# Sixty kept edge groups in place of sixty-six in the four-head graph attention sums

## The chip, the cores and the metric

The kernel runs on one core of a Trainium2 chip. The core has a matrix engine (PE, with its weight loads as PEld), a vector engine (DVE), a scalar engine (ACT), a general engine (POOL) and a queue engine (SP). SP, ACT and POOL can issue transfers, and all transfers share 16 DMA engines. The metric is the device time of one execution in microseconds, as the median of several runs. Lower is better.

## The reference

Two graph layers run over 3125 nodes and 50000 edges, sorted by destination. Each has an attention over edges, a linear attention over all nodes and a mixture of experts. The change touches the first attention pass of the second layer, which has four heads of 128 columns:

```python
h = (x @ W).reshape(N, heads, out_c)
a_src = jnp.einsum('nhc,hc->nh', h, att_src)
a_dst = jnp.einsum('nhc,hc->nh', h, att_dst)
e = jax.nn.leaky_relu(a_src[src] + a_dst[dst], NEG_SLOPE)
...
msg = h[src] * alpha[:, :, None]
out = jax.ops.segment_sum(msg, dst, num_segments=N)
```

For every edge a row of `h` is fetched by the edge's source, scaled by the edge's weight for each head, and added into the row of the edge's destination. Four heads of 128 columns and one more column each make a row of 516 floats, 2064 bytes.

## The kernel before

The edges stand in 196 blocks of 256. A block can span several tiles of 128 destination nodes, so the work is cut into `W` = 220 edge groups (block and tile; called w in the code), and each has two halves of 128 edges (`SUB` = 2). The sum of one group is a matrix product: a one-hot matrix of destinations (128 edges by 128 nodes) times the 128 scaled rows, done for two halves and two banks of 261 columns, and added to the tile's accumulator in SBUF.

The rows of a group come into SBUF by one of two ways.

- **Direct rows.** POOL issues two indirect gathers (L1616, one for each half of 128 rows) from `table1` in DRAM within the sums themselves.
- **Kept rows.** For the groups in the list `STAGED`, POOL issues the same two gathers earlier, in other stages (L1173), and a queue writes the rows as one dense block of 516 KB to `kept1` in DRAM (L1183). In the sums SP reads that block back with one plain transfer (L1604).

`STAGED` holds the groups with w % 10 in (2, 5, 8), 66 of 220. The first `FIRST` = 16 of them are gathered and stored in the linear attention of this layer, those up to `EARLY` = 56 (40 groups) in the score stage, and the remaining 10 in the softmax stage. In each of these stages five buffers (`KQ`) turn over: POOL's gather of group n waits until the store of group n - 5 has landed.

The stages run one after another with a barrier between them. Those that matter here, in order:

1. The score stage, `edge_scores_l1`. For 110 pairs of edge groups SP loads a block of one-hot matrices (`hots`, 128 KB, ten buffers), PE multiplies, DVE masks (L1315) and reduces (L1321). Beside it POOL gathers kept groups and ACT's queue stores them.
2. The softmax stage, `segment_softmax`, with 10 more kept groups.
3. The sums, `aggregate`. POOL issues the direct gathers in group order into `QD` = 7 slots; a slot is free once PE has summed the group that held it. SP loads kept blocks into `QS` = 3 slots. ACT writes five more columns into each group's rows (L1640) and scales the second half by the edge weights (L1644). DVE writes the one-hot matrices (L1668, `QH` = 5 buffers), scales the first half (L1673) and adds PE's result to the accumulator (L1682). PE multiplies (L1659).

In the sums POOL, SP, ACT and PE have straight code for 220 groups. DVE runs a loop (L1692) with `J1` = 20 groups in its body, since the tile of a group is only known at run time. The order of DVE's work is written out: one-hot and message of group w + 2, then the addition of group w. `J1` has to be a multiple of the period of `STAGED`, and the counts per turn of the body of both slot rings have to come out whole; that is where the constants 2 * 16 in `landed` come from.

Of the kernel before, what the change touches and what calls it, by code (L numbers as in the profile page):

```python
# [36 lines left out]
W = NB + NT - 1  # L37
SUB = EB // P
# [11 lines left out]
H1, DH1 = 4, 128  # L50
# [4 lines left out]
WSP = 448  # L55
C0, C1, C2 = 16, 32, 112
ROW0 = H0 * (DH0 + 1)
J1 = 20
STAGED = [w for w in range(W) if w % 10 in (2, 5, 8)]
FIRST = {H1: 16, 1: 0}  # L60
EARLY = {H1: 56, 1: 58}
KQ = 5
STAGED_B = [b for b in range(NB) if b % 3 == 1]
RING = 37
# [1091 lines left out]
def staged(H):  # L1156
    return STAGED if H == H1 else STAGED_B

# [5 lines left out]
def gather_rows(pool, K, table, rows, windows, s_free, sources=None):  # L1164

    Q = rows.shape[1]
    sources = K.src_col if sources is None else sources
    for n, w in enumerate(windows):
        q = n % Q
        if n >= Q:  # L1170
            pool.wait_ge(s_free[q], 16 * (n // Q))
        for s in range(SUB):
            pool.indirect_dma_start(rows[:, q, s, :], None, table,  # L1173
                                    bass.IndirectOffsetOnAxis(ap=sources[:, w * SUB + s:w * SUB + s + 1], axis=0)).then_inc(K.gath[q], 16)
# [19 lines left out]
def edge_scores_l1(prog, K, name, H, C, RW, table, kept, A):  # L1194
# [4 lines left out]
    with Stage(prog, name) as st:  # L1199
# [30 lines left out]
        turns = W // (G * QL)  # L1230
        first, early = FIRST[H], EARLY[H]
        L = WSP // C * P
# [147 lines left out]
def segment_softmax(prog, K, name, H, C, keep_max=None, RW=0, table=None, kept=None, A=None):  # L1380
# [8 lines left out]
    with Stage(prog, name) as st:  # L1389
# [18 lines left out]
        s_free = [st.sem(f"free{q}") for q in range(KQ)]  # L1408
        early, late = (EARLY[H], len(staged(H)) - EARLY[H]) if table is not None else (0, 0)
        if late:  # L1410
# [147 lines left out]
def aggregate(prog, K, name, H, RW, table, kept, acc, extra):  # L1558
# [4 lines left out]
    B = 1 if RW <= 512 else 2  # L1563
    part = -(-(RW + X) // B)
    with Stage(prog, name) as st:
        U2, QH, J = 4, 5, J1
        QS, QD = 3, 7
        size = SUB * B * part
        HALF = 1 if B > 1 else SUB
        al = K.al[:, 0:WS * H].rearrange("p (s h) -> p s h", h=H)  # L1570
# [7 lines left out]
        s_gath, gathered = K.gath, list(K.gathered)  # L1578
        s_rows = [st.sem(f"rows{q}") for q in range(QS)]
# [5 lines left out]
        if by_act:  # L1585
            away = st.sbuf("away", [P, 2, SUB, P])
            one = st.sbuf("one", [P, 1])
        direct = [w for w in range(W) if w not in STAGED]
        rows, landed = {}, {}
        for n, w in enumerate(direct):  # L1590
            rows[w] = slots[n % QD]
            landed[w] = (s_gath[n % QD], gathered[n % QD] + 16 * SUB * (n // QD + 1), 2 * 16 * SUB)
        for n, w in enumerate(STAGED):
            rows[w] = slots[QD + n % QS]
            landed[w] = (s_rows[n % QS], 16 * (n // QS + 1), 2 * 16)
        per_ready = 1 if by_act else 2
        block = st.block()

        @block.sync
        def _(sp):  # L1600
            for n, w in enumerate(STAGED):
                if n >= QS:
                    sp.wait_ge(s_sum, STAGED[n - QS] + 1)
                sp.dma_start(rows[w][:, :, 0:RW], kept[n * EB:(n + 1) * EB, :].rearrange("(s p) r -> p s r", p=P)).then_inc(s_rows[n % QS], 16)  # L1604
# [775 lines left out]
def linear_attention_l1(prog, K, A):  # L2380

    KD = LH * LD
    with Stage(prog, "mix1") as st:
# [33 lines left out]
        def _(pool):  # L2417
            st.clear_stale(pool)
            gather_rows(pool, K, K.table1, held, STAGED[0:FIRST[H1]], s_free)

# [581 lines left out]
def stages(prog, K, A, out):  # L3002

    order_edges(prog, K, A)
    items_project_l0(prog, K, A)
    linear_attention_l0(prog, K, A)
    edge_scores_l0(prog, K, A)
    segment_softmax(prog, K, "soft0", H0, C0, A=A)
    aggregate_l0(prog, K)
    finish_route_l0(prog, K, A)  # L3010
    experts_l0(prog, K, A)
    join_project_l1(prog, K, A)
    linear_attention_l1(prog, K, A)
    for H, C, RW, table, kept, acc in ((H1, C1, H1 * (DH1 + 1), K.table1, K.kept1, K.acc1),
                                       (1, C2, D + 1, K.table2, K.kept2, K.acc2)):
        keep = K.al[:, WSP * H:WSP * (2 * H + 1)].rearrange("p (s h) -> p s h", h=H + 1)
        edge_scores_l1(prog, K, f"score_h{H}", H, C, RW, table, kept, A)
        segment_softmax(prog, K, f"soft_h{H}", H, C, keep, RW, table, kept)
        if H == H1:
            aggregate(prog, K, f"sum_h{H}", H, RW, table, kept, acc, keep)  # L3020
            middle_l1(prog, K, A)
        else:
            aggregate_one(prog, K, table, kept, acc, keep)
    finish_route_l1(prog, K, A)
    experts_l1(prog, K, A)
    combine_l1(prog, K, out)
# [126 lines left out]
```

## Time and profile before

| What | Value |
| --- | --- |
| Median of three runs | 3053.57 us (3051.1 to 3061.77) |
| The profiled execution | 3050.74 us, its span 3049.0 us |
| PE, share of the span busy | 2105.7 us, 69% |
| DVE | 2085.5 us, 68% |
| POOL | 1440.7 us, 47% |
| ACT | 827.2 us, 27% |
| Score stage, up to its last store | about 1493 to 1640 us from the span's start |
| Softmax stage | about 1665 to 1711 us |
| The sums | about 1711 to 2143 us |

Busy shares of the whole span mix stages with different limits, so the table is only a map. The page's chain of work that ended last covers only the final 44 us of the span and says nothing of these stages. What a change here is worth has to be read from the views of each stage: busy times in a stretch, who waited for whom in it, and the instructions in order of time.

### The profile page before, as it was taken

How to read it: one execution, taken by the hardware profiler on the slowest of the kernel's cores; microseconds unless marked ns; L12 is line 12 of the kernel's file. 1: busy time of each engine (PE TensorE's matmuls, PEld its weight loads, DVE VectorE, ACT ScalarE, POOL GpSimd, SP SyncE). 2: the span in 40 equal slices, each digit the busy share in tenths (PEclk: the TensorE clock that was granted, in tenths of full speed). 3: DMA queues.
4: the chain of work that ended last, by engine and by line, in shares of the span. 5: the costliest groups of instructions: out<-in, count | busy, mean ns of one | idle time of the engine just before them, and what ended most of it. 6: DMA issues, size and time to landing. Idle time of an engine off the chain costs nothing. (4 is left out here: it accounts for less than half of the span.)

```text
span 3049.0 us, 51563 instructions
## 1 busy us (share of the span) xinstructions
PE 2105.7 (69%) x11892; PEld 1580.5 (52%) x11893; DVE 2085.5 (68%) x4524; ACT 827.2 (27%) x2459; POOL 1440.7 (47%) x1486
## 2 busy tenths in 40 slices
PE   2634878757887389948665499999756188887372
PEld 2322434445665355624565377787645177776252
DVE  7496888888888343353478688888677277778442
ACT  2314444431001212124200467676500000001110
POOL 2477777700000310130553777777357677771234
PEclk9866998979998599979777699999856599998586
DMA  4777999935775278843997788898589645550085
GB/s 151 208 205 218 269 269 270 271 139 172 229 232 149 98 256 271 271 125 118 340 393 263 238 278 281 277 287 275 137 285 269 190 130 158 159 148 20 35 257 175
DMA packets 447837, 649.13 MB, mean 213 GB/s; under 512 B 67552, under 2 KB 328286, under 8 KB 447123
## 3 DMA queue, kind: packets, MB, share of 16 engines
q1 hardware_dynamic: 329747, 351.62, 37.0%
q0 software_dynamic: 82640, 248.85, 27.6%
q10 hardware_dynamic: 35296, 46.90, 4.5%
q8 instruction: 61, 1.00, 0.1%
q14 instruction: 93, 0.76, 0.1%
HBM read 478.83 MB, written 169.68 MB: 213 GB/s over the span
## 5 line engine op out<-in xcount | busy, mean ns | idle before, releaser
L1616 POOL DMA_INDIRECT wide<-table,src_col x264 | 277.9, 1053 | 80.7 <-issue 73.3
L1777 PE MATMUL sum_h_ps<-wide,sum_h_hot 128*128 x880 | 254.1, 412 | 75.4 <-DVE wide L1802 45.6
L1037 POOL DMA_INDIRECT arena_b<-table,al x272 | 258.1, 949 | 89.2 <-issue 85.2
L1753 POOL DMA_INDIRECT wide<-table,al x262 | 257.9, 984 | 85.8 <-issue 58.8
L1659 PE MATMUL sum_h_ps<-wide,sum_h_hot 128*128 128x261 f32 x1056 | 253.4, 389 | 37.2 <-ACT wide L1644 21.2
L1885 PE MATMUL sum_ps<-wide,sum_hot 128*128 128x264 f32 x880 | 211.9, 394 | 52.4 <-DVE sum_hot L1895 27.5
L1659 PEld LDWEIGHTS sum_h_ps<-wide,sum_h_hot 128*128 128x128 f32 x1056 | 197.3, 191 | 85.2 <-issue 29.7
L1173 POOL DMA_INDIRECT wide<-table,src_col x132 | 138.6, 1050 | 198.1 <-issue 134.1
L1885 PEld LDWEIGHTS sum_ps<-wide,sum_hot 128*128 128x128 f32 x880 | 163.8, 191 | 100.4 <-issue 74.9
L1058 PE MATMUL score_ps_hd<-wide,score_hot 128*128 x1320 | 209.5, 301 | 0.0
L1777 PEld LDWEIGHTS sum_h_ps<-wide,sum_h_hot 128*128 128x128 f32 x880 | 155.2, 197 | 92.8 <-issue 79.7
L1114 DVE TENSOR_TENSOR wide<-wide,score_ps_hd 128x528 f32<-128x528 f32 x220 | 153.3, 697 | 37.8 <-PE score_ps_hd L1058 32.9
L1899 DVE TENSOR_TENSOR wide<-wide,al 128x528 f32<-128x528 f32 x220 | 154.4, 702 | 32.8 <-DMA wide<-edge_h 32.2
L1068 ACT ACTIVATE wide<-score_ps_en 128x512 f32<-128x512 f32 x220 | 130.5, 594 | 147.6 <-PE score_ps_en L1054 147.1
L1644 ACT ACTIVATE wide<-wide,al 128x129 f32<-128x129 f32 x528 | 167.3, 388 | 0.0
L797 POOL DMA_INDIRECT wide<-table,al x120 | 124.1, 1034 | 91.0 <-issue 90.7
L1659 PE MATMUL sum_h_ps<-arena_b,sum_h_hot 128*128 128x261 f32 x704 | 166.2, 383 | 0.1
L1682 DVE TENSOR_TENSOR wide<-wide,sum_h_ps 128x522 f32 x220 | 152.3, 692 | 19.5 <-issue 13.6
L1054 PE MATMUL score_ps_en<-enc_rows,score_attr 30*128 30x256 bf16 x440 | 91.5, 290 | 104.2 <-DVE score_hot L1107 35.8
L1173 POOL DMA_INDIRECT wide<-table,al x130 | 125.2, 963 | 73.4 <-issue 53.2
L1058 PEld LDWEIGHTS score_ps_hd<-wide,score_hot 128*128 128x128 bf16 x1320 | 118.9, 104 | 72.9 <-issue 52.5
L1973 POOL MEMSET route_ones<- 128x128 f32 x1 | 0.4, 400 | 325.7 <-POOLq L127 325.7
(537 smaller groups left out, 4991.9 us busy)
## 6 DMA issues: line engine op xcount, KB each, us to landing
wide<-edge_h SPq DMA_DIRECT2D x220, 264.0 KB, 3.0
edge_h<-arena_b SPq DMA_DIRECT2D x68, 528.0 KB
arena_b<-kept SPq DMA_DIRECT2D x66, 516.0 KB, 5.2
wide<-edge_rows SPq DMA_DIRECT2D x110, 256.0 KB, 4.7
score_h_hot<-hots SPq DMA_DIRECT2D x220, 128.0 KB
kept<-wide ACTq DMA_DIRECT2D x40, 516.0 KB, 8.5
wide<-kept SPq DMA_DIRECT2D x65, 257.0 KB
wide<-in_f_w SPq DMA_DIRECT2D x16, 1024.0 KB, 10.0
```

What stands on the lines that cost most here:

```text
L1037: pool.indirect_dma_start(rows[:, q, k, :], None, K.table0[:, :], bass.IndirectOffsetOnAxis(ap=K.src_blk[:, g * GS + k:g * GS + k + 1], ax ...
L1058: ins = pe.matmul(ps_hd[:, m, s, 0:D + H], lhsT=hot[:, q, edges[s]], rhs=near[:, window, c, :], start=(c == 0), stop=(c == 2))
L1114: dve.tensor_tensor(prod[:, w % U3, :].rearrange("p (s d) -> p s d", s=SUB), enc[:, m, :].rearrange("p (s d) -> p s d", s=SUB), ps_hd[:, m ...
L1173: pool.indirect_dma_start(rows[:, q, s, :], None, table, bass.IndirectOffsetOnAxis(ap=sources[:, w * SUB + s:w * SUB + s + 1], axis=0)).th ...
L1616: pool.indirect_dma_start(rows[w][:, s, 0:RW], None, table, bass.IndirectOffsetOnAxis(ap=K.src_col[:, w * SUB + s:w * SUB + s + 1], axis=0 ...
L1644: ins = act.activation(cols, cols, ACT.Copy, scale=al[:, w * SUB + 1, h:h + 1])
L1659: ins = pe.matmul(ps[:, u, b, 0:part], lhsT=hot[:, w % QH, s, :], rhs=rows[w][:, s, b * part:(b + 1) * part], start=(s == 0), stop=(s == S ...
L1682: dve.tensor_tensor(out, out, ps[:, j % U2, :, 0:part], ALU.add).then_inc(s_acc, 1)
L1753: pool.indirect_dma_start(ring[:, b % RING, s, :], None, table, bass.IndirectOffsetOnAxis(ap=K.src_blk[:, b * SUB + s:b * SUB + s + 1], ax ...
L1777: pe.matmul(ps[:, u, 0:RW], lhsT=hot[:, q, s, :], rhs=ring[:, bass.ds(places[j % 4], 1), s, :].rearrange("p a r -> p (a r)"), start=(s == ...
L1885: ins = pe.matmul(ps[:, bass.ds(banks[j % 4], 1), 0:ROW0].rearrange("p a c -> p (a c)"), lhsT=hot[:, q, s, :], rhs=rows[:, q, s, :], start ...
L1899: dve.tensor_tensor(view, view, al[:, bass.ds(w * SUB, SUB), :].unsqueeze(3).broadcast_to([P, SUB, H, R]), ALU.mult).then_inc(s_msg, 1)
```

## The change

The list of kept groups becomes w % 11 in (2, 6, 9), 60 groups. `FIRST` stays 16, `EARLY` becomes 50, so that the score stage keeps 34 groups in place of 40 and the softmax stage still 10. The sums have 160 direct groups in place of 154, eight direct slots in place of seven, and four one-hot buffers in place of five. The loop body of DVE covers 44 groups in place of 20.

```diff
-J1 = 20
-STAGED = [w for w in range(W) if w % 10 in (2, 5, 8)]
+J1 = 44
+STAGED = [w for w in range(W) if w % 11 in (2, 6, 9)]
 FIRST = {H1: 16, 1: 0}
-EARLY = {H1: 56, 1: 58}
+EARLY = {H1: 50, 1: 58}
...
-        U2, QH, J = 4, 5, J1
-        QS, QD = 3, 7
+        U2, QH, J = 4, 4, J1
+        QS, QD = 3, 8
...
-            landed[w] = (s_gath[n % QD], gathered[n % QD] + 16 * SUB * (n // QD + 1), 2 * 16 * SUB)
+            landed[w] = (s_gath[n % QD], gathered[n % QD] + 16 * SUB * (n // QD + 1), 4 * 16 * SUB)
...
-            landed[w] = (s_rows[n % QS], 16 * (n // QS + 1), 2 * 16)
+            landed[w] = (s_rows[n % QS], 16 * (n // QS + 1), 4 * 16)
```

POOL's row of instructions at the score stage, as a piece of the difference (x80 means eighty in a row, two for each group):

```order
 L1261 UNCONDITIONAL_BRANCH
 L120 ISA
-L1173 DMA wide<-table,src_col 128x516 x80
+L1173 DMA wide<-table,src_col 128x516 x68
 L127 UNCONDITIONAL_BRANCH
 L1433 UNCONDITIONAL_BRANCH
```

Twelve gathers have left the score stage; ACT's queue has 34 stores there in place of 40 (L1183).

POOL's row at the start of the sums, before the change (`wide` holds six of the direct slots, `arena_b` the rest):

```order
L120 ISA
L1611 MEMSET wide 128x2 x6
L1611 MEMSET arena_b 128x2 x4
L1616 DMA wide<-table,src_col 128x516 x12
L1616 DMA arena_b<-table,src_col 128x516 x2
```

And after it:

```order
L120 ISA
L1611 MEMSET wide 128x2 x6
L1611 MEMSET arena_b 128x2 x5
L1616 DMA wide<-table,src_col 128x516 x12
L1616 DMA arena_b<-table,src_col 128x516 x4
```

A turn of the slots is now 16 gathers for eight groups in place of 14 for seven; the pattern goes on to 320 gathers in place of 308. SP's row at the same stage has 60 loads of kept blocks (L1604) in place of 66. The work of DVE, ACT and PE for a group is the same and in the same order; the loop of DVE, from its first instruction to its branch back, is 472 instructions long in place of 220.

## Rows read from the trace of the kernel before

**Rows 1.** Busy us of the engines (and counts) in stretches: scores, their end, softmax, sums
```profile
core 0: us, PE busy (x) PEld busy (x) DVE busy (x) ACT busy (x) POOL busy (x), PEclk, DMA share, GB/s
...
1493.00:1640.00 147.00, 94.73 (x1479) 85.14 (x1478) 114.94 (x193) 0.00 (x0) 76.77 (x80) 0.73 1.04 385
1640.00:1665.00 25.00, 14.06 (x298) 13.16 (x296) 24.26 (x57) 0.00 (x0) 0.00 (x0) 0.84 0.31 98
1665.00:1712.00 47.00, 13.13 (x48) 6.59 (x46) 25.97 (x21) 11.47 (x24) 31.99 (x30) 0.50 0.71 225
1712.00:2143.00 431.00, 401.07 (x1760) 330.38 (x1760) 362.26 (x661) 297.40 (x1101) 328.65 (x308) 0.98 0.86 271
```

**Rows 2.** Groups of POOL in the sums: busy us, mean ns, idle before, releasers
```profile
L1616 POOL DMA_INDIRECT wide<-table,src_col x264 | 277.9, 1053 | 80.7 <-issue 73.3 <-PE sum_h_ps L1659 7.3
L1616 POOL DMA_INDIRECT arena_b<-table,src_col x44 | 50.7, 1153 | 13.4 <-issue 11.6 <-PE sum_h_ps L1659 1.8
```

**Rows 3.** The line of the direct gathers: ns min/median/max, first and last start
```profile
L1616 POOL DMA_INDIRECT wide<-table,src_col x264: 942/948/6483, 1712.3 to 2130.4; - x132
L1616 POOL DMA_INDIRECT arena_b<-table,src_col x44: 942/1241/1450, 1733.5 to 2133.6; - x44
```

**Rows 4.** Waits of POOL in the sums: total us, times, longest us
```profile
POOL wide L1616 <- issue: 73.3, 240, 0.5
...
POOL wide L1616 <- PE sum_h_ps L1659: 7.3, 24, 0.3
```

**Rows 5.** Waits of DVE in the sums
```profile
DVE wide L1673 <- DMA wide<-table,src_col: 44.1, 52, 4.3
...
DVE sum_h_hot L1668 <- issue: 3.4, 1, 3.4
```

**Rows 6.** Sums in order of time, five instructions: start us, us, engine, operation
```profile
1711.30 6.68 DVE L1687 TENSOR_TENSOR wide<-eps 128x6264 f32<-128x6264 f32 x1 [16.69 <-DMA wide<-edge_h]
...
1712.33 6.48 POOL L1616 DMA_INDIRECT wide<-table,src_col  x1 [0.53 <-issue]
...
1915.15 0.94 POOL L1616 DMA_INDIRECT wide<-table,src_col  x1 [0.30 <-issue]
...
1924.03 0.69 DVE L1673 TENSOR_TENSOR arena_b<-arena_b,al 128x516 f32<-128x516 f32 x1
...
1924.29 1.24 POOL L1616 DMA_INDIRECT arena_b<-table,src_col  x1 [0.30 <-issue]
```

**Rows 7.** The end of the sums in order of time: last gather, last addition
```profile
2133.57 0.95 POOL L1616 DMA_INDIRECT arena_b<-table,src_col  x1 [0.30 <-issue]
...
2141.45 0.70 DVE L1682 TENSOR_TENSOR wide<-wide,sum_h_ps 128x522 f32 x1 [0.91 <-PE sum_h_ps L1659]
```

**Rows 8.** The group of POOL's gathers in the score stage, as in Rows 2
```profile
L1173 POOL DMA_INDIRECT wide<-table,src_col x80 | 76.8, 960 | 72.3 <-DMA kept<-wide 47.1 <-issue 14.3 <-POOLq L127 10.9
```

**Rows 9.** POOL in the score stage in order of time: first and last gather
```profile
1493.44 0.94 POOL L1173 DMA_INDIRECT wide<-table,src_col  x1 [10.86 <-POOLq L127]
...
1630.74 0.95 POOL L1173 DMA_INDIRECT wide<-table,src_col  x1 [0.30 <-issue]
```

**Rows 10.** The longest wait of PE in the score stage, from 1493 to 1640 us
```profile
PE score_h_ps L1293 <- DMA score_h_hot<-hots: 38.2, 54, 1.5
```

**Rows 11.** DVE's masks in order of time: 1, 91, 92 and 110 of 110
```profile
1511.90 0.62 DVE L1315 TENSOR_TENSOR wide<-score_h_ps,arena_b 128x448 f32<-128x448 f32 x1 [1.59 <-PE score_h_ps L1295]
...
1639.42 0.62 DVE L1315 TENSOR_TENSOR wide<-score_h_ps,arena_b 128x448 f32<-128x448 f32 x1
...
1640.57 0.62 DVE L1315 TENSOR_TENSOR wide<-score_h_ps,arena_b 128x448 f32<-128x448 f32 x1
...
1659.60 0.62 DVE L1315 TENSOR_TENSOR wide<-score_h_ps,arena_b 128x448 f32<-128x448 f32 x1
```

**Rows 12.** Transfers from 1493 to 1640 us: all; stores: count, KB, us to landing
```profile
DMA packets 31543, 56.56 MB, mean 385 GB/s; under 512 B 3504, under 2 KB 16244, under 8 KB 31401
...
kept<-wide ACTq DMA_DIRECT2D x40, 516.0 KB, 8.5
```

## The prediction, made before the run

> **What bounds the kernel now.** The page's chain of waits ends in the last 44 us, so I read the two stages that the change touches one by one: busy times in stretches [rows 1], then who waited in each, then single instructions. The reader should look for the engine that never rests.
>
> In the sums that is POOL. Its gathers run from 1712.33 to 2133.57 + 0.95 = 2134.52 us [rows 6, 7], 422.2 us for 308. Their busy time is 277.9 + 50.7 = 328.6 us, and the idle time ahead of them 80.7 + 13.4 = 94.1 us [rows 2]; together 422.7, the whole stretch. The idle time is no wait: it is 0.305 us ahead of every gather, and where PE's freeing of a slot is named as releaser it is never over 0.3 us either [rows 4]. So POOL issues without a pause, and slots never hold it up. The others wait for it: DVE 44.1 us for rows that have not landed [rows 5]. PE is busy 401 of 431 us [rows 1], but busy PE is pipelined and modelled, and DVE's and PE's last work ends 7.6 us behind POOL's last gather (2141.45 + 0.70 against 2134.52 [rows 7]), as a short pipeline behind its source would. The sums last as long as their gathers.
>
> A gather takes 0.948 us in the median [rows 3], with the gap 1.253. The mean is longer: 328.6 - 308 x 0.948 = 36.6 us are on top. How shows in the order of time [rows 6]: the first gather starts while DVE clears the accumulator (L1687, until 1717.98) and takes 6.48 us, ending after it; the one at 1924.29 starts 0.26 us into a message multiply (L1673) and takes 1.24; the one at 1915.15 has none beside it and takes 0.94. So gathers that start inside certain DVE operations are held: 5.5 us in the first, 31 us spread over the other 307, or 0.10 each.
>
> In the score stage the transfers are full: share 1.04, 385 GB/s, until 1640 us, then 0.31 [rows 1]. PE waits 38.2 us for the blocks of one-hot matrices [rows 10], and DVE, which ends the stage, waits for PE. When stores and gathers are over, DVE runs without a pause: 18 masks from 1640.57 to 1659.60, 1.057 us each; before that 90 masks took 1511.90 to 1639.42, 1.417 us each [rows 11].
>
> **The change part by part.**
>
> *Twelve gathers more in the sums.* 160 direct groups in place of 154, two gathers each: 12 x 1.253 = 15.0 us on the path that sets the stage's end. Nothing hides them, for POOL has no pause. The holds I leave at their 36.6 us in all: they come from 220 message multiplies, whose number stays, and as groups come more slowly a gather is less likely to start inside one. If the holds went by gathers, the mean of the 307, (422.2 - 6.8) / 307 = 1.353, would hold: 16.2 us. Downwards, fewer holds could take back at most those 31 us (a rival below). I take +15.0, with 12 to 17 as its near bounds.
>
> The Trainium skill ("SBUF — State Buffer", section "Who interferes with whom") says that a DVE instruction with two SBUF inputs contends with a GpSimd instruction that reads SBUF, and adds, as inferred, that tensor_tensor was not seen to stall transfers issued by GpSimd. The held gathers here agree with the first and speak against the second. By the first the holds belong to DVE's work and the term is 15.0; by the second they would be the gathers' own and it would be 16.2.
>
> *Six kept groups less in the score stage.* 80 gathers become 68, 40 stores 34. POOL waits there for stores (47.1 us [rows 8]), and 40 groups take 1493.44 to 1631.69, 3.46 us each [rows 9]; six less end 20.7 us earlier. In these 20.7 us DVE goes at 1.057 instead of 1.417 us a pair: the gain is 20.7 x (1 - 1.057 / 1.417) = 5.3 us. It cannot be less than nothing, since only work leaves. As upper bound, the bytes: six groups read and stored are 6 x 2 x 516 KB = 6.3 MB, at 385 GB/s [rows 12] 16.5 us, if all of that became the stage's. I take -5.3, since the last 19 us of the stage are already at DVE's own pace and cannot shrink.
>
> *Six loads less on SP, the same bytes in all.* A load of a kept group is replaced by gathers of the same rows; SP waits for slots only. Nothing is queued behind it. 0.
>
> *Ten late groups in the softmax stage* (1665 to 1712 us [rows 1]) and 16 early ones stay in number. 0.
>
> *Eight direct slots, four one-hot buffers.* POOL was never held by seven slots, so an eighth gives nothing. DVE writes the one-hot of group w + 2 after the addition of w - 1, when PE is through with w - 1 and all before; the fourth buffer back held w - 2. No wait is added. 0; the one memset more costs less than a gather's gap.
>
> *The loop body of 472 instructions in place of 220.* The trace shows one stall of DVE's instruction supply, 3.4 us at the entry of the loop, and none at its branches back [rows 5]. A body of the new length isn't in the trace, so each of the three branches back (four turns in the loop) costs between 0 and 3.4 us of DVE, 10.2 in all. DVE isn't the bound, though. What a late DVE delays is a slot's release. Eight slots turn over in 16 x 1.353 = 21.6 us; a slot is needed from its first gather to its group's addition, about 1.25 + (2141.45 - 2133.57) = 9.1 us by the last group [rows 7]. Some 12 us of cover hide 3.4. 0; if the cover is gone, 10.2.
>
> **The sum.** 15.0 - 5.3 = +9.7 us. On the profiled execution (3050.74 us; span 3049.0) this gives 3060.4; that execution lies 2.8 below the median of the runs (3053.57), from which it gives 3063.3. I put the median at 3062.
>
> A difference of about 0.3%, 9.2 us, is what a measurement of this kernel can tell from no change. The forecast, slower, stands right on that line.
>
> **The rivals.**
>
> *The score stage gives back all its bytes (not slower).* Place: PE's wait for one-hot blocks. With the transfers full until 1640, 6.3 MB less might bring the whole stage forward 16.5 us: 15.0 - 16.5 = -1.5, on the scale of the 3062 above 3051. It decides when the stores end later than DVE's last wait, so that DVE's free stretch stays 19 us long. For it: the share of 1.04. Against: DVE has to do its 110 pairs at 1.057 or more whatever the transfers do, and blocks gain only as much as DVE loses now.
>
> *DVE's loop stalls at each turn and the cover does not hold (slower).* 3 x 3.4 = 10.2 us on top: 3072. Part of it may come another way: a DVE that catches up has its multiplies closer together and holds more gathers. For it: the stall at entry. Against: the cover above. The Trainium skill ("Runtime: NRT & Kernel Launch", section "Instruction fetch mechanics") says that an engine keeps two pages of 256 instructions, fetched in sequence, and that a taken branch out of them waits for a fetch. The old body fits in one page, the new one takes both; no trace so far shows which way this falls.
>
> *The holds go away (faster).* The starts of gathers fall differently against the multiplies; if all 31 us vanished, 15.0 - 31 - 5.3 = -21.3, 3031; half of them, 3046. For it: 0.94 is the time of a gather that is left alone. Against: nothing in the change takes multiplies away or shifts them.
>
> *The sums do not follow the gathers.* If PE sets the pace, twelve more gathers fill pauses, and only the score stage counts: 3062 - 15.0 = 3047. Against: POOL has no pauses.
>
> **How the numbers follow.** The sum as worked out: 66%, with some 4 us either way, so it falls about evenly on the two sides of the line: 36% slower by over 0.3%, 30% within. Score stage gives back all: 12%, within. Loop stalls: 13%, slower. Holds go away: 5%, faster. Sums not bound by gathers: 4%, within. Faster 5%, within 46%, slower 49%. The range of 3053 to 3070 leaves out the holds, most of the score stage's full return, half of the loop's stalls, some 2 in 10.
>
> **What would show it.** In the profile after: 320 gathers in the sums with idle gaps of 0.3 us and no long wait for PE, from first to last some 437 us; a median of 0.95 us; DVE still waiting for landed rows. The score stage's last gather some 20 us nearer its first, and DVE's free stretch at 1.06 us some 35 masks long in place of 19. DVE idle for instructions once, or four times, at the loop. The prediction is wrong if gathers wait for slots, if the score stage shortens by far more than 5 us, or if the mean gather is no longer about 1.06 us.

## The result: slower by 0.6%, and what the profile after shows

| | kernel before | changed kernel |
|---|---|---|
| median of 11 runs of each, us | 3046.17 (3033.96 to 3061.77) | 3065.7 (3056.51 to 3072.87) |
| ratio, 95% interval | | 1.0059 (1.0039 to 1.0078) |
| profiled execution, its span, us | 3050.74, 3049.0 | 3062.84, 3061.1 |
| score stage, us | 172.1 | 165.6 |
| softmax stage, us | 46.6 | 46.7 |
| sums, us | 432.0 | 462.0 |

A stage is counted from its own start to the start of the next (POOL's first instruction in each, L120). By the ratio the change costs 0.0059 x 3046 = 18 us, where 9.7 were forecast. In the two profiled executions the score stage gives back 6.5 us and the sums cost 30. The stages that the change doesn't touch are 11.5 us shorter together (30.0 - 6.5 + 0.1 - 12.1) in this one execution of the changed kernel; over the 14 profiles of this study the time ahead of the score stage runs from 1488.2 to 1496.0 us and that behind the sums from 898.6 to 907.1, and this execution lies at the low end of both. So sizes in whole are taken from the medians and places from the profiles.

The changed kernel by stretches, as in [rows 1]: scores while POOL gathers, the rest of the scores, softmax, sums.

```profile
core 0: us, PE busy (x) PEld busy (x) DVE busy (x) ACT busy (x) POOL busy (x), PEclk, DMA share, GB/s
1488.00:1617.00 129.00, 87.95 (x1327) 80.95 (x1328) 101.98 (x170) 0.00 (x0) 68.17 (x68) 0.68 1.03 382
1617.00:1654.00 37.00, 22.19 (x451) 19.93 (x448) 36.26 (x80) 0.00 (x0) 0.00 (x0) 0.91 0.31 91
1654.00:1700.00 46.00, 13.25 (x48) 6.69 (x47) 25.39 (x20) 10.74 (x23) 31.63 (x20) 0.50 0.71 230
1700.00:2162.00 462.00, 411.10 (x1760) 336.23 (x1760) 367.04 (x661) 300.43 (x1101) 355.05 (x331) 0.96 0.82 253
```

The score stage did what the forecast said. Its first and last gather, and three of VectorE's masks (the first, the 77th and the 110th), in order of time:

```profile
1489.07 0.94 POOL L1173 DMA_INDIRECT wide<-table,src_col  x1 [10.29 <-POOLq L127]
...
1506.67 0.62 DVE L1315 TENSOR_TENSOR wide<-score_h_ps,arena_b 128x448 f32<-128x448 f32 x1 [1.59 <-PE score_h_ps L1295]
...
1603.51 0.94 POOL L1173 DMA_INDIRECT wide<-table,src_col  x1 [0.30 <-issue]
...
1613.82 0.61 DVE L1315 TENSOR_TENSOR wide<-score_h_ps,arena_b 128x448 f32<-128x448 f32 x1
...
1648.70 0.62 DVE L1315 TENSOR_TENSOR wide<-score_h_ps,arena_b 128x448 f32<-128x448 f32 x1
```

From first to last gather 114.4 us against 137.3 before [rows 9]. The last 34 masks run without a pause, (1648.70 - 1613.82) / 33 = 1.057 us apart, the same pace as the last 19 before [rows 11].

The sums did not. The two groups of POOL's gathers, as in [rows 2]:

```profile
L1616 POOL DMA_INDIRECT wide<-table,src_col x240 | 269.5, 1123 | 73.3 <-issue 65.7 <-PE sum_h_ps L1659 7.6
L1616 POOL DMA_INDIRECT arena_b<-table,src_col x80 | 85.1, 1064 | 24.4 <-issue 23.2 <-PE sum_h_ps L1659 1.2
```

The idle time is 73.3 + 24.4 = 97.7 us for 320 gathers, still 0.305 each: POOL issues without a pause as before, and no wait for a slot appears. But a gather takes 354.6 / 320 = 1.108 us in the mean where it took 1.067. I call *held time* what the gathers after the first take beyond 0.945 us each (the first starts in VectorE's clearing of the accumulator and is 5.2 to 5.5 us over in each kernel): 354.6 - 302.4 - 5.2 = 47.0 us, where rows 2 give 32.0 in the same way. So the 30 us are 12 x 1.25 = 15 for the gathers, and 15 for holds that were forecast to stay.

VectorE's waits in the sums, as in [rows 5], name the second thing that is new:

```profile
DVE wide L1673 <- DMA wide<-table,src_col: 43.6, 43, 4.4
...
DVE sum_h_hot L1668 <- issue: 16.2, 4, 4.8
```

It now stalls for instructions four times, 16.2 us, where it stalled once for 3.4: at the entry and at each of three branches back. In order of time, around the first branch back (L1673 is the message multiply, L1668 the one-hot):

```profile
1802.39 0.69 DVE L1673 TENSOR_TENSOR wide<-wide,al 128x516 f32<-128x516 f32 x1
...
1807.34 0.95 POOL L1616 DMA_INDIRECT wide<-table,src_col  x1 [0.30 <-issue]
1808.29 0.42 DVE L1668 TENSOR_TENSOR sum_h_hot<-iota_row,rel_col 128x256 f32<-128x256 f32 x1 [4.31 <-issue]
...
1820.47 0.69 DVE L1673 TENSOR_TENSOR arena_b<-arena_b,al 128x516 f32<-128x516 f32 x1
1820.51 1.46 POOL L1616 DMA_INDIRECT wide<-table,src_col  x1 [0.30 <-issue]
...
1822.24 0.69 DVE L1673 TENSOR_TENSOR arena_b<-arena_b,al 128x516 f32<-128x516 f32 x1
1822.28 1.46 POOL L1616 DMA_INDIRECT wide<-table,src_col  x1 [0.30 <-issue]
```

During the stall the gathers run free and POOL loses nothing. It loses later: multiplies follow each other every 1.77 us, one gather starts 0.04 us into each of them and takes 1.46 us in place of 0.945. Eleven such steps stand in a row from 1816.9 us on. There are four rows of steps of 1.74 to 1.80 us in the trace, at 1816.9, 1905.2, 1997.5 and 2104.3 us, of 11, 10, 11 and 5 steps; the first three each begin 12 to 15 us after the start of the multiply step that the stall lengthened. The four hold gathers for 18.5 us of the 47.0. The trace of before has no row of three or more.

### The profile page after: what moved, and what is told of

Its sections match the earlier page's. It is cut to its first block and busy times, and to the rows that moved or that the text cites. A ratio compares the mean times of both kernels' runs of the same rounds, so it can differ in the third digit from the quotient of the medians.

```text
span 3061.1 us, 51420 instructions
## 1 busy us (share of the span) xinstructions
PE 2108.4 (69%) x11892; PEld 1586.4 (52%) x11893; DVE 2091.6 (68%) x4524; ACT 828.7 (27%) x2459; POOL 1456.1 (48%) x1487
## 5 line engine op out<-in xcount | busy, mean ns | idle before, releaser
L1616 POOL DMA_INDIRECT wide<-table,src_col x240 | 269.5, 1123 | 73.3 <-issue 65.7
L1659 PE MATMUL sum_h_ps<-wide,sum_h_hot 128*128 128x261 f32 x960 | 233.8, 394 | 44.2 <-ACT wide L1644 21.0
L1659 PEld LDWEIGHTS sum_h_ps<-wide,sum_h_hot 128*128 128x128 f32 x960 | 183.2, 194 | 89.0 <-DVE wide L1673 34.1
L1173 POOL DMA_INDIRECT wide<-table,src_col x120 | 130.0, 1084 | 199.0 <-issue 148.4
L1777 PEld LDWEIGHTS sum_h_ps<-wide,sum_h_hot 128*128 128x128 f32 x880 | 155.4, 197 | 91.6 <-issue 78.7
L1659 PE MATMUL sum_h_ps<-arena_b,sum_h_hot 128*128 128x261 f32 x800 | 192.2, 390 | 13.8 <-DVE arena_b L1673 11.7
L1058 PE MATMUL score_ps_hd<-wide,score_hot 128*128 x1320 | 201.5, 293 | 0.0
L1659 PEld LDWEIGHTS sum_h_ps<-arena_b,sum_h_hot 128*128 128x128 f32 x800 | 153.0, 193 | 43.8 <-DVE arena_b L1673 17.5
L1119 DVE TENSOR_REDUCE al<-wide 128x16 f32<-128x528 f32 x220 | 153.0, 696 | 0.0
## 6 DMA issues: line engine op xcount, KB each, us to landing
score_h_hot<-hots SPq DMA_DIRECT2D x220, 128.0 KB, 12.3
```

Source lines behind the costliest of these rows:

```text
L1058: ins = pe.matmul(ps_hd[:, m, s, 0:D + H], lhsT=hot[:, q, edges[s]], rhs=near[:, window, c, :], start=(c == 0), stop=(c == 2))
L1119: dve.tensor_reduce(al[:, w * SUB:(w + 1) * SUB, :], prod[:, w % U3, :].rearrange("p (s h r) -> p s h r", s=SUB, h=H), AX, ALU.add).then_i ...
L1173: pool.indirect_dma_start(rows[:, q, s, :], None, table, bass.IndirectOffsetOnAxis(ap=sources[:, w * SUB + s:w * SUB + s + 1], axis=0)).th ...
L1616: pool.indirect_dma_start(rows[w][:, s, 0:RW], None, table, bass.IndirectOffsetOnAxis(ap=K.src_col[:, w * SUB + s:w * SUB + s + 1], axis=0 ...
L1659: ins = pe.matmul(ps[:, u, b, 0:part], lhsT=hot[:, w % QH, s, :], rhs=rows[w][:, s, b * part:(b + 1) * part], start=(s == 0), stop=(s == S ...
L1777: pe.matmul(ps[:, u, 0:RW], lhsT=hot[:, q, s, :], rhs=ring[:, bass.ds(places[j % 4], 1), s, :].rearrange("p a r -> p (a r)"), start=(s == ...
```

## The experiments

Each kernel was run beside the kernel before; a ratio is against that. For the sums, the length of the stage and the held time in one profiled execution are given.

| kernel | groups kept, form of VectorE's loop | sums, us | held, us | ratio, 95% interval |
|---|---|---|---|---|
| before | 66, turns of 20 | 432.0 | 32.0 | 1 |
| after | 60, turns of 44 | 462.0 | 47.0 | 1.0059 (1.0039 to 1.0078) |
| before_body40 | 66, turns of 40 | 444.3 | 44.3 | 1.0025 (1.0010 to 1.0040) |
| before_straight | 66, no loop | 451.8 | 51.7 | 1.0050 (1.0032 to 1.0068) |
| list_straight | 60, no loop, 7 slots, 5 one-hots | 458.2 | 41.2 | 1.0066 (1.0048 to 1.0084) |
| after_straight | 60, no loop | 463.7 | 49.1 | 1.0070 (1.0042 to 1.0097) |
| after_gaps | 60, no loop, 3 pauses put in | 463.7 | 49.6 | 1.0070 (1.0049 to 1.0092) |
| after_short | 60, turns of 44, multiply cut | 425.1 | 4.1 | one execution, 3036.6 us |
| before_psum | 66, no loop, weights in PSUM | 407.7 | 5.0 | 0.9905 (0.9886 to 0.9924) |
| after_psum | 60, no loop, weights in PSUM | 422.2 | 5.6 | 0.9922 (0.9906 to 0.9938) |
| after_pad256 | 60, no loop, 0.34 us more work a group | 437.7 | 20.4 | 0.9988 (0.9976 to 1.0000) |
| after_pad128 | 60, no loop, 0.20 us more work a group | 470.9 | 56.8 | 1.0097 (1.0073 to 1.0121) |
| before_loads | 66, no loop, register loads added | 495.6 | 30.7 | 1.0197 (1.0178 to 1.0215) |
| after_loads | 60, no loop, register loads added | 496.4 | 29.7 | 1.0181 (1.0162 to 1.0200) |

The score stage takes 161.7 to 167.7 us in the kernels with 60 groups kept and 170.6 to 172.5 in those with 66.

### Is it the loop? Straight code, pauses, and a long body on the old list

after_straight takes the loop out of VectorE's part of the sums:

```diff
-            turns = W // J
-            with aligned(dve, 0, turns - 1) as i:
-                for j in range(J):
-                    message(i + (j + 2) // J, (j + 2) % J)
-                    add(i, j)
...
+            for w in range(W):
+                if w + 2 < W:
+                    message(0, w + 2)
+                add(0, w)
```

> The changed kernel with DVE's 220 groups in the sums written out as straight code, so that no branch back is left. Loop theory: the 472-instruction body stalls DVE 4.3 to 5.0 us at each of its three branches back; DVE then runs without a pause at PE's pace, and POOL's gathers start inside its message multiplies one after the other. Without the branches the sums fall from 462 us to 445 to 455, holds from 47 us (without the first gather) to 32 to 38, and the whole stands at +0.1 to +0.4% of before. Rival, the pattern: the holds come with 3 of 11 and 320 gathers whatever the loop does; the sums stay at 458 to 462 us and the whole at +0.6%.

Sums 463.7 us, held 49.1, ratio 1.0070: no stall is left, and nothing is won. As far as this run went, the loop was cleared.

after_gaps is after_straight with a reduction into a tile that nobody reads (4.8 us) behind groups 43, 87 and 131, so that VectorE pauses where the loop would branch.

```diff
...
+                if w in (43, 87, 131):
+                    dve.tensor_reduce(idle[:, :], K.al[:, 0:1480].unsqueeze(1).broadcast_to([P, 3, 1480]), AX, ALU.max)
...
```

> As the changed kernel with straight code, but with three reductions of about 4.6 us on DVE (one input, result unused) after groups 43, 87 and 131, where the loop branched back. If lateness of DVE is what costs, by its catching up, the sums are as long as with the loop, 455 to 462 us, though no instruction is fetched anew. If the fetch itself costs (its transfers, or the branch), the sums are as with straight code alone, 445 to 455 us.

463.7 us and 49.6 held, longer than either view had expected: three pauses add nothing to straight code, which already had as many holds. But the pauses do make rows. Behind the first one (L1674 is the multiply here):

```profile
1808.93 4.78 DVE L1697 TENSOR_REDUCE sum_h_idle<-al 128x3 f32<-128x4440 f32 x1
...
1824.82 0.69 DVE L1674 TENSOR_TENSOR arena_b<-arena_b,al 128x516 f32<-128x516 f32 x1
1824.86 1.47 POOL L1617 DMA_INDIRECT wide<-table,src_col  x1 [0.30 <-issue]
```

Rows of 9, 10 and 11 steps begin at 1821.3, 1909.1 and 2009.1 us, at groups 50, 93 and 142, where the changed kernel's begin at groups 50, 93 and 138; after_straight has no row near them. VectorE takes no branch here, so being late is enough to start a row. The total stays because other holds go: gathers in steps of 1.5 to 1.6 us hold 8.0 us in place of 14.3.

before_body40 puts the long body on the old list: 66 groups kept, seven slots, five one-hot buffers, turns of 40 groups in place of 20.

```diff
-J1 = 20
+J1 = 40
...
-            with aligned(dve, 0, turns - 1) as i:
+            with aligned(dve, 0, 4) as i:
...
+            for w in range(4 * J, W):
+                if w + 2 < W:
+                    message(0, w + 2)
+                add(0, w)
...
```

> The kernel before (66 kept groups, 308 gathers) with DVE's loop body of 40 groups in place of 20, four turns, the last 60 groups as straight code. Loop theory: three branches back stall 4 to 5 us each, the gathers after each are held, and the sums grow from 432 us by 7 to 15. Rival, the pattern: no stall that matters, sums 430 to 434 us, whole within 0.1% of before.

It stalls at its branches back like the changed kernel and is slower by 0.25%, 7.6 us; sums +12.3 us, held time 44.3, also +12.3. So one part of the change, alone, brings four fifths of the 15 us of new holds. One thing goes with the long body: the last 60 groups are straight code, where before has 20 and the changed kernel 44. Of the 12.3 us, 8.5 fall in the first 160 groups and 3.7 in those 60. Its waits and its order of time:

```profile
DVE sum_h_hot L1668 <- issue: 14.9, 4, 4.1
```

```profile
1885.32 0.43 DVE L1668 TENSOR_TENSOR sum_h_hot<-iota_row,rel_col 128x256 f32<-128x256 f32 x1 [4.09 <-issue]
...
1890.59 0.69 DVE L1673 TENSOR_TENSOR arena_b<-arena_b,al 128x516 f32<-128x516 f32 x1
1890.86 1.25 POOL L1616 DMA_INDIRECT wide<-table,src_col  x1 [0.30 <-issue]
...
1892.14 0.70 DVE L1673 TENSOR_TENSOR wide<-wide,al 128x516 f32<-128x516 f32 x1
1892.41 1.24 POOL L1616 DMA_INDIRECT wide<-table,src_col  x1 [0.30 <-PE sum_h_ps L1659]
...
1898.45 0.69 DVE L1673 TENSOR_TENSOR wide<-wide,al 128x516 f32<-128x516 f32 x1
1898.61 1.35 POOL L1616 DMA_INDIRECT wide<-table,src_col  x1 [0.30 <-issue]
...
1901.98 0.69 DVE L1673 TENSOR_TENSOR arena_b<-arena_b,al 128x516 f32<-128x516 f32 x1
1902.03 1.47 POOL L1616 DMA_INDIRECT wide<-table,src_col  x1 [0.30 <-issue]
```

Here the holds can be read as a rule. A gather that starts 0.27 us into a multiply takes 1.25 us (0.30 held), at 0.16 us it takes 1.35 (0.40), at 0.05 us 1.47 (0.52). Start and hold add up to 0.57 us each time: **the gather goes on when 0.57 of the multiply's 0.69 us have passed**. Over all 172 gathers of after_straight that start in a multiply the means agree: 0.49 held for starts at 0.05 to 0.10 us, 0.30 at 0.20 to 0.30, 0.01 from 0.50 on. (Of the starts in the first 0.03 us none is held, from 0.04 us on all of them are: the gather that comes first is let through.)

From this follows when the next gather starts, wherever in the multiply the held one began: 0.57 + 0.945 + 0.305 = 1.82 us after the multiply's start (median in the trace of after 1.813, over the 128 gathers held by more than 0.05 us). If the next multiply starts sooner than that, the gather falls into it, and it is held too unless it comes in the first 0.03 us. That puts the boundary near 1.82 - 0.03 = 1.79 us, and the eleven traces with the whole multiply and both inputs in SBUF bear it out: behind a held gather the next one is held in all 541 steps of 1.5 to 1.78 us, in 44 of 51 from 1.78 to 1.79, and in 1 of 26 from 1.79 to 1.82. **Multiplies in step at under 1.79 us keep the gathers in step with them: one gather for each, at the multiplies' pace, in place of one each 1.25 us.** The hold is then what the step has over 1.25 us: VectorE catching up has steps of 1.55 us (0.30 held), VectorE waiting for TensorE steps of 1.77 us (0.51 held; in the rows TensorE ends a group every 1.766 us, and each addition starts 0.16 us behind it). The chain ends when the landed rows are used up and a multiply has to wait. A stall of 4 us is what starts a long one: three or four gathers land unhindered meanwhile, VectorE then has rows in store, and goes without landing waits for 14 to 18 groups.

Neither view of the loop had it whole: it does cost, in long turns; straight code, which has no stalls, gets as many holds from somewhere else.

### Do the multiplies hold the gathers?

after_short is the changed kernel with the multiply cut to the first column of each head; the other columns of that half stay unweighted.

```diff
-                view = rows[j][:, 0:HALF, 0:RW].rearrange("p s (h r) -> p (s h) r", h=H)
+                view = rows[j][:, 0:HALF, 0:RW].rearrange("p s (h r) -> p (s h) r", h=H)[:, :, 0:1]
...
```

> The changed kernel with its loop, the message multiply of DVE cut to the first column of each head (128 x 4 in place of 128 x 516), so that 128 of 129 columns of each group's first half stay unscaled. If gathers are held by this multiply, its holds shrink with its length (0.69 us to about 0.1): mean gather 0.95 to 1.0 us, 320 x 1.26 = 403 us from first to last, sums 415 to 430 us. If they are held by anything else (ring space, full transfers), the mean stays at 1.07 to 1.1 us and the sums at 445 us or more.

Held time 4.1 us with 320 gathers, sums 425.1 us: the multiply it is. But it takes work away too, so the next pair doesn't. before_psum and after_psum copy the head weights once into two spare PSUM banks (three PSUM pairs for the sums in place of four); the multiply is as long as before and has one input in SBUF, not two. Both are in straight code.

```diff
-        U2, QH, J = 4, 5, J1
+        U2, QH, J = 3, 5, J1
...
+        hw = st.psum("hw", [P, 1024])
...
-                dve.tensor_tensor(view, view, al[:, bass.ds(w * SUB, HALF), :].rearrange("p s h -> p (s h)").unsqueeze(2).broadcast_to([P, HALF * H, RW // H]),
+                dve.tensor_tensor(view, view, weights(w, 1).unsqueeze(2).broadcast_to([P, HALF * H, RW // H]),
...
+            for k in range(4):
+                dve.tensor_copy(weights(60 * k, min(60, W - 60 * k)).rearrange("p (s h) -> p s h", h=H), al[:, 120 * k:min(120 * k + 120, WS):2, :]).then_inc(s_one, 1)
```

> The kernel before in straight code, with the head weights that the message multiply reads copied once into two spare PSUM banks (three PSUM pairs for the sums in place of four), so that the multiply has one SBUF input and one from PSUM; nothing else is changed and nothing is left out. If the holds come from the multiply's two inputs in SBUF, gathers lose nearly all of their 32 us, and the sums end about 20 us earlier, near 410 to 415 us, where TensorE (220 groups of 1.758 us) takes over as the bound. If the holds come from the write of the rows, or from any VectorE work, they stay and the sums stay at 430 us or more.

> The same on the changed kernel (60 kept groups, eight slots, four one-hot buffers). If the holds are gone in both, the difference of the sums to before_psum is the bare price of twelve more gathers: 12 x 1.25 = 15 us where the gathers are the bound, 0 to 5 us where TensorE is. The changed kernel would be at 0 to +9 us against before_psum in whole, since its scores end 6.5 us earlier. If the holds stay, sums 455 us or more.

Both came out as expected, and better. POOL's groups in the sums of before_psum, the sums as one stretch, and a gather that starts 0.17 us into a multiply (L1677 there):

```profile
L1617 POOL DMA_INDIRECT wide<-table,src_col x264 | 259.3, 982 | 80.6 <-issue 71.8 <-PE sum_h_ps L1660 8.8
...
L1617 POOL DMA_INDIRECT arena_b<-table,src_col x44 | 42.3, 962 | 13.4 <-issue 10.4 <-PE sum_h_ps L1660 3.0
```

```profile
1709.00:2117.00 408.00, 391.49 (x1760) 333.78 (x1760) 367.41 (x665) 295.87 (x1101) 301.96 (x318) 0.98 0.88 286
```

```profile
1854.72 0.69 DVE L1677 TENSOR_TENSOR wide<-wide,sum_h_hw 128x516 f32<-128x516 f32 x1
1854.89 0.95 POOL L1617 DMA_INDIRECT arena_b<-table,src_col  x1 [0.30 <-issue]
```

The same start cost 0.40 us in before_body40 and costs nothing here. So it is the second SBUF input of this multiply, not the write and not VectorE being busy. Two SBUF inputs alone don't say how long a hold is: the one-hot has two as well, and 48 gathers that started in it here were held by 0.09 us in the mean. Against its own control, before_straight, the sums fall by 44.1 us; the kernel is 0.95% faster than the kernel before, 27.2 us by medians (3022.83 against 3049.98), and the fastest of this study. With the holds gone the two lists show the bare price: sums 14.5 us longer with twelve more gathers, scores 8.6 shorter, 4.5 us in whole by the medians (3027.34 - 3022.83), though the two intervals overlap.

### What the list costs in straight code

before_straight is the kernel before without the loop, list_straight that with the list of 60 alone.

```diff
-STAGED = [w for w in range(W) if w % 10 in (2, 5, 8)]
+STAGED = [w for w in range(W) if w % 11 in (2, 6, 9)]
...
-EARLY = {H1: 56, 1: 58}
+EARLY = {H1: 50, 1: 58}
...
```

> The kernel before (list, seven slots, five one-hot buffers kept), with VectorE's loop in the sums of the four-head pass written out in full, as in after_straight. It is the control for that run. Theory A, the list itself brings the holds (the message multiplies of eight direct groups in eleven fall behind TensorE's pace, then gathers and multiplies run in step): here the old list is in straight code, so the sums stay at 432 us (+-4), held time of the gathers after the first near 32 us, the time within 0.2% of before. Theory B, what counts is the form of the loop (twenty groups with cheap branches back keep the multiplies out of step, every other form does not): sums near 444 to 450 us, held time 44 us or more, the time 10 to 16 us above before, and of the 18 us of the change only the bare gathers, 5 to 15 us, belong to the list.

> The kernel before with the new list alone (60 kept groups, the scores' count of early groups with it), in straight code; seven slots for direct rows and five one-hot buffers as before. Theory A (list): as after_straight, sums 460 to 466 us, held time 47 to 50 us; slots and one-hot buffers have no part in it. Rival (the four one-hot buffers bring VectorE back into step with TensorE): sums 445 to 450 us, held time 35 to 40 us.

The control fell to theory B: the old list in straight code has 51.7 us of held time, more than the changed kernel, and is 0.5% slower than its own loop of twenty. list_straight met neither of its expectations, with 458.2 us and 41.2 held. Between these two the list costs 3.1 us (3068.6 - 3065.52), less than the intervals can tell from nothing. Slots and one-hot buffers (after_straight against list_straight) can't be told from nothing either.

Where straight code differs from the loop can be read behind a multiply that waited for its rows. In before_straight:

```profile
1861.92 0.70 DVE L1673 TENSOR_TENSOR wide<-wide,al 128x516 f32<-128x516 f32 x1 [0.27 <-DMA wide<-table,src_col]
1862.09 1.34 POOL L1616 DMA_INDIRECT wide<-table,src_col  x1 [0.30 <-issue]
...
1863.70 0.69 DVE L1673 TENSOR_TENSOR arena_b<-arena_b,al 128x516 f32<-128x516 f32 x1
1863.74 1.47 POOL L1616 DMA_INDIRECT wide<-table,src_col  x1 [0.30 <-issue]
```

The step is 1.78 us, under the boundary: one hold leads to the next. In the kernel before the same step is 1.89 us (median of 46), since its addition starts 0.24 us behind such a multiply and not 0.14: the next gather starts in time, ahead of the next multiply. Of these steps 3 of 46 are under 1.79 us in before, 39 of 43 in before_straight.

### Is there such a boundary? More work, less time

If chains need steps under 1.8 us, VectorE must get *slower* to free the gathers. after_pad256 is after_straight with the group's one-hot made a second time into a buffer that nobody reads; after_pad128 makes half of it.

```diff
...
+                if w >= 2:
+                    dve.wait_ge(s_spare, w - 1)
+                dve.tensor_tensor(spare[:, w % 2, 0:2, :], K.iota_row[:, :].unsqueeze(1).broadcast_to([P, 2, P]),
+                                  K.rel_col[:, bass.ds(w * SUB, 2)].unsqueeze(2).broadcast_to([P, 2, P]), ALU.is_equal).then_inc(s_spare, 1)
...
```

> after_straight with work added: ahead of every message multiply VectorE makes the group's one-hot a second time into a scratch buffer that nobody reads (128x256, 0.42 us, of which 0.08 overlaps: 0.34 us more per group, 75 us more VectorE work in all). Theory (step): in all traces a gather that starts s us into a multiply ends s-independently, held until 0.57 us of the multiply have passed (hold = 0.57 - s), so the next gather starts 1.82 us after that multiply's start; it falls into the next multiply, and is held again, only when multiplies follow each other in less than 1.82 us. Catch-up steps of 1.55 and 1.77 us do; with the added work the shortest step is 1.55 + 0.34 = 1.89 us, so chains of held gathers can't form: held time falls from 49 us to 15 or less, and the sums get shorter in spite of the added work, 463.7 -> 435 to 448 us (VectorE 220 x 1.89 = 416 plus 20 to 30 at the ends and waits). Rival (a gather is held the more, the more VectorE works): held time 50 us or more, sums 470 us or more.

> The same with half of the added work: only the first 128 columns of the one-hot are made twice (about 0.28 us, 0.20 us more per group, 44 us more in all). By the step theory the shortest step of the multiplies is then about 1.75 us, still under 1.82: gathers stay in step, each held 1.82 - 1.75 + ... = about 0.5 us, so held time stays at 45 us or more and the sums at 460 us or more: worse than with twice the added work. Rival (added work only loosens VectorE and gathers in proportion): between after_straight and after_pad256.

Gathers (min/median/max ns, by the line of POOL) and the sums as one stretch, after_pad256:

```profile
L1618 POOL DMA_INDIRECT wide<-table,src_col x240: 945/967/6147, 1705.5 to 2125.3; - x120
L1618 POOL DMA_INDIRECT arena_b<-table,src_col x80: 945/967/1585, 1726.5 to 2130.4; - x80
```

```profile
1704.00:2142.00 438.00, 417.76 (x1760) 318.40 (x1760) 425.99 (x881) 297.64 (x1101) 328.45 (x331) 0.98 0.85 267
```

after_pad128, and one step of a chain in it:

```profile
L1618 POOL DMA_INDIRECT arena_b<-table,src_col x80: 942/1370/1465, 1728.9 to 2168.4; - x80
```

```profile
1707.00:2177.00 470.00, 411.46 (x1760) 332.74 (x1760) 405.15 (x881) 300.09 (x1101) 364.65 (x330) 0.97 0.81 248
```

```profile
1841.03 0.69 DVE L1679 TENSOR_TENSOR wide<-wide,al 128x516 f32<-128x516 f32 x1
1841.09 1.44 POOL L1618 DMA_INDIRECT wide<-table,src_col  x1 [0.30 <-PE sum_h_ps L1661]
```

The step theory stands on both sides. With 0.20 us more a group, 102 of 219 steps are under 1.79 us, all but the first of them at 1.75 or more, where a hold is 0.5 us, and the sums lengthen to 470.9; with 0.34 us more, one is, VectorE is busy 426 of 438 us, and the sums are 26 us *shorter* than without any padding. The two runs put the boundary between 1.75 and 1.89 us; the traces above put it at 1.79. Held time of after_pad256 is 20.4 us where 15 or less was expected. 13.4 us of it is one chain of 21 gathers from 2057.45 us on, with steps of 1.885 us and 0.64 us held: its gathers start 0.07 to 0.08 us *ahead* of the multiply, inside the useless one-hot. So a gather can also be caught just before the multiply starts, and a chain run at longer steps. The start alone doesn't decide that: 89 other gathers of this run start equally far ahead at the same steps and take 0.97 to 0.99 us. What sets the 21 apart stays open.

### A test that missed its aim

before_loads and after_loads were to lengthen only the step behind a landing, by reading the register of the addition three times.

```diff
...
-                window = dve.value_load(K.window[0:1, bass.ds(w, 1)], min_val=0, max_val=NT - 1)
+                for again in range(3):
+                    window = dve.value_load(K.window[0:1, bass.ds(w, 1)], min_val=0, max_val=NT - 1)
...
```

> before_straight with the window's register load written three times ahead of each add (two of them useless). In the traces the step from a multiply that waited for its rows to the next one is 1.89 us in the kernel before's loop of twenty groups and 1.78 us in straight code, since the add behind it starts 0.24 us after the multiply in the loop and 0.14 us in straight code; the boundary at which a held gather meets the next multiply is 1.82 us. Step theory: the added loads lengthen that one step past 1.82 us and are hidden elsewhere, so the straight code behaves as the loop did: held time 51.7 -> 28 to 38 us, sums 451.8 -> 428 to 438 us, the time within 0.3% of before. Rival (the step after a landing doesn't matter; straight code is worse for another reason): held time 45 us or more, sums 448 us or more.

> The same on the changed kernel in straight code: no branches back, no instruction stalls, and the step after a landing past 1.82 us. If the chains of held gathers came with the form of the code, the new list keeps only the bare price of its twelve gathers, 12 x 1.25 = 15 us on the sums of before_loads, less the 6 to 8 us of the shorter scores: sums 443 to 453 us, the time 5 to 10 us above before_loads, which is what the prediction's sum said. If the new list brings chains of its own, sums 460 us or more and the time 15 us or more above before_loads.

```profile
1712.00:2207.00 495.00, 448.38 (x1760) 318.47 (x1760) 371.06 (x661) 297.29 (x1101) 327.72 (x318) 0.98 0.78 236
```

```profile
POOL wide L1616 <- PE sum_h_ps L1659: 45.7, 47, 1.5
```

The loads were not hidden: the addition starts 0.49 us behind every multiply, all steps but the first are over 2 us, VectorE's sequence sets the pace, and for the first time POOL waits for slots. Held time fell to 30.7 and 29.7 as the step theory says, but the sums came to 495.6 and 496.4 us where 428 to 438 and 443 to 453 were expected. That is no test of the step behind a landing, and whether that step alone makes the 20 us between before and before_straight was not settled. Chance gave another answer: with the sums bound by VectorE, twelve more gathers cost them 0.8 us, and the list of 60 comes out 3.6 us ahead (3113.25 against 3116.82), 0.16% of the kernel before.

## Why the prediction was right in direction, and half in size

**The score stage: right.** -5.3 forecast, -6.5 in the profiles, -6.0 to -8.9 in the pairs of like form (60 kept against 66). The mechanism is the one named: gathers end earlier, and 34 masks (35 forecast) at 1.057 us in place of 19.

**The bare gathers: right.** +15.0 forecast; 14.5 in the pair without holds. POOL never paused and never waited for a slot, so the eighth slot and the four one-hot buffers at 0 hold too, as far as can be told.

**"The holds I leave at their 36.6 us": the step that failed.** They were 52.2 with the first gather's. The reason given, that slower groups make a start inside a multiply less likely, treats starts as independent. They are not: a held gather puts the next one 1.82 us behind the multiply's start. What counts is not how many steps are short enough (under 1.79 us are 111 in the changed kernel and 108 in the kernel before), but how long they are and whether they stand in a row. In the changed kernel 54 steps are 1.74 to 1.80 us long, with 0.5 us of hold each in a row; in the kernel before 12 are, and 82 are at 1.5 to 1.6 us, with 0.3 us when one is caught.

**"The loop body: 0": wrong, by the wrong question.** The stalls came and were longer than the bound: (16.2 - 2.8) / 3 = 4.5 us each where at most 3.4 was allowed (2.8 us is the stall at the entry). The cover was real: no slot was late. I asked only what a late VectorE delays, not what it does while it catches up. The rival on the loop had that in a half sentence ("a DVE that catches up has its multiplies closer together and holds more gathers") and no price. before_body40 gives one: 7.6 us (3 to 12 by its interval). With it the sum is 9.7 + 7.6 = 17.3 us, and 18 were measured; with so wide an interval, so close a meeting is partly luck.

So the two forecast terms were right and the third, at zero, is the missing half. The remainder, 0.59% less 0.25%, is 10 us for the list and the rest, with long turns on both sides; in straight code the list costs 3 us, without holds 4.5, and where VectorE binds it gains. What the list costs thus depends on how the multiplies step, and the forecast's +9.7 for it is borne out for long turns only: the new list was not run with short turns, so that the two parts simply add up is not shown. Why straight code steps as it does is read from the traces; that this alone makes its holds stays open.

**The median: luck.** 3062 was forecast and 3065.7 came, but the kernel before measured 3046.17 beside it where the forecast started from 3053.57. The rise was 18 us, not 9.7.

**The criterion** that the forecast gave against itself, a mean gather that is no longer about 1.06 us, is the one that turned up: 1.108.

The Trainium skill ("SBUF — State Buffer", section "Who interferes with whom") says that a VectorE instruction with two SBUF inputs contends with a GpSimd instruction that reads SBUF, and reports a probe in which tensor_tensor did not stall transfers, with a reason that it marks as inferred. The runs agree with the first (5.0 us held with one input in SBUF, 51.7 with two) and not with the second as far as indirect gathers go. The prediction weighed the same two sentences for the number of holds, and the choice between them did not matter: neither says that holds come in chains.

The Trainium skill ("Runtime: NRT & Kernel Launch", section "Instruction fetch mechanics") gives two pages of 256 instructions. By the trace a turn of the changed loop has 514 instructions (44 register checks among them), not 472, and 514 are more than two pages; a turn of before_body40 has 469, which would fit if its first one opens a page, and it stalled at every branch back too.

## What to carry to other kernels

Where one engine is held while another runs a certain instruction, write down when the held one starts again and compare that with the other's period: a period a little shorter than this return time locks the two, and the hold is paid anew every time. Look then for the cheap way out of the conflict itself (here one operand in PSUM, 0.95%), before counting how many of the held instructions there are. And an engine that is off the path and "covered" still has a price when it catches up: ask what its burst collides with.

## What the runs showed of the hardware that was not expected

- An indirect gather of 128 rows that starts within a 128x516 tensor_tensor with both inputs in SBUF resumes 0.57 us into its 0.69, whatever its own start from 0.04 us on; with one input in PSUM (before_psum, after_psum) it isn't held.
- The one-hot, a tensor_tensor with both inputs broadcast from SBUF, hardly holds a gather: 0.09 us in the mean and 0.20 at most over 48 gathers that started in it in before_psum.
- A turn of 514 instructions by the trace (after) stalls VectorE for 4.3 to 4.8 us at each branch back and one of 469 (before_body40) for 4.0 to 4.1. With one of 238 (before) the instruction behind the branch comes some 0.25 us late and VectorE doesn't idle; straight code shows no stall at all.
- Two more register loads ahead of an addition put it 0.49 us behind the multiply in place of 0.14: about 0.18 us each, hidden by nothing.
- 75 us more of VectorE work (220 x 0.34) made the sums 26 us shorter (after_pad256 against after_straight).
